# One stage for both input projections, the mixing layer's matrices folded into one, and a dense product with preloaded matrices

## The reference, cut to what matters

```python
xn = _layernorm(x, axis=-1)
x = x + _L0_gnn_ref(xn, edge_index, W, att_src, att_dst, bias) + _L0_mix_ref(xn[None], ...)[0]

def _L0_gnn_ref(x, ...):
    h = (x @ W).reshape(N, 4, 64)
    a_src = jnp.sum(h * att_src[None], axis=-1)
    a_dst = jnp.sum(h * att_dst[None], axis=-1)
    ...   # attention over the edges, + bias, relu

def _L0_mix_ref(x, ...):                 # 8 heads of 32, rank 4
    h = layernorm(x, ln1_g, ln1_b)
    xm = h @ Wx + bx                     # 256 x 256
    q = softmax(xm @ Wq, axis=-1)        # per head, 32 x 4
    k = softmax(xm @ Wk, axis=-2)
    v = xm @ Wv                          # per head, 32 x 32
    attn = (q @ (k.T @ v)) @ Wo + bo
    fx = attn + x
    h2 = layernorm(fx, ln2_g, ln2_b)
    m = gelu(h2 @ W1 + b1) @ W2 + b2     # 256 x 1024, 1024 x 256
    return m + fx
```

## Time and profile before

| | us |
|---|---|
| median of three runs | 5163.15 |
| lowest, highest | 5148.55, 5177.3 |
| the profiled execution | 5160.48 |
| its span (first to last instruction) | 5158.8 |
| busy in it: PE, PEld | 4545.8, 4131.4 |
| busy in it: DVE, ACT, POOL | 3174.7, 2848.2, 1417.0 |

### The profile page before, as it was taken

One profiled execution on the slowest core, in us unless ns is written; L12 is line 12 of the kernel. 1 busy time (PEld: TensorE's weight loads), 2 busy tenths in 40 slices (PEclk: granted clock), 3 DMA queues, 4 the chain that ended last, 5 costly groups with the idle time before them and its releaser, 6 DMA issues. The chain is left out here.

```text
span 5158.8 us, 91254 instructions
## 1 busy us (share of the span) xinstructions
PE 4545.8 (88%) x34042; PEld 4131.4 (80%) x34042; DVE 3174.7 (62%) x2705; ACT 2848.2 (55%) x3889; POOL 1417.0 (27%) x1134
## 2 busy tenths in 40 slices
PE   3555668999999769987799999989999999799989
PEld 3443457999999769964599999978999999688755
DVE  6884322888788531126388888844888888255323
ACT  2662223777777433323077787753778777344332
POOL 0001000122122012210136656640666666100000
PEclk9776779999999789988899999999999999899989
DMA  3881011333333155540144344422443443454100
GB/s 93 137 135 20 3 44 26 97 98 98 86 96 94 56 175 185 184 135 11 39 114 103 101 102 106 103 68 76 105 106 93 106 106 94 118 135 111 29 17 20
DMA packets 199348, 467.51 MB, mean 91 GB/s; under 512 B 108564, under 2 KB 145951, under 8 KB 177016
## 3 DMA queue, kind: packets, MB, share of 16 engines
q1 hardware_dynamic: 179120, 428.36, 32.9%
q0 software_dynamic: 14016, 28.15, 2.2%
q10 hardware_dynamic: 5879, 6.17, 0.4%
HBM read 389.74 MB, written 72.83 MB: 90 GB/s over the span
## 5 line engine op out<-in xcount | busy, mean ns | idle before, releaser
L1161 PE MATMUL g2a_pso<-HX,g2a_wt 125*125 125x129 f32 x5000 | 603.4, 274 | 8.2 <-ACT g2a_wt L1045 4.4
L1161 PE MATMUL g1a_pso<-HX,g1a_wt 125*125 125x129 f32 x5000 | 602.7, 274 | 4.4 <-ACT g1a_wt L1045 3.3
L1161 PE MATMUL g0a_pso<-HX,g0a_wt 125*125 125x65 f32 x5000 | 593.5, 273 | 4.7 <-ACT g0a_wt L1045 3.3
L1161 PEld LDWEIGHTS g0a_pso<-HX,g0a_wt 125*125 125x125 f32 x5000 | 583.6, 193 | 5.0 <-ACT g0a_wt L1045 3.5
L1161 PEld LDWEIGHTS g2a_pso<-HX,g2a_wt 125*125 125x125 f32 x5000 | 576.8, 189 | 8.9 <-ACT g2a_wt L1045 4.8
L1161 PEld LDWEIGHTS g1a_pso<-HX,g1a_wt 125*125 125x125 f32 x5000 | 576.4, 189 | 4.9 <-ACT g1a_wt L1045 3.5
L1045 ACT ACTIVATE g0a_wt<-g0a_pst 125x1000 f32<-125x1000 f32 (+1 forms) x300 | 312.0, 1040 | 197.9 <-PE g0a_pst L1148 197.9
L978 DVE SCALAR_TENSOR_TENSOR g0a_x<-g0a_als,g0a_cd,HX 125x3125 f32<-125x3125 f32 x100 | 347.5, 3475 | 108.5 <-PE g0a_pst L1148 99.3
L978 DVE SCALAR_TENSOR_TENSOR g2a_x<-g2a_als,g2a_cd,g2a_as 125x3125 f32<-125x3125 f32 x100 | 357.7, 3577 | 83.2 <-PE g2a_pst L1148 73.2
L978 DVE SCALAR_TENSOR_TENSOR g1a_x<-g1a_als,g1a_cd,g1a_as 125x3125 f32<-125x3125 f32 x100 | 358.3, 3583 | 81.1 <-PE g1a_pst L1148 70.6
L1045 ACT ACTIVATE g1a_wt<-g1a_pst 125x1000 f32<-125x1000 f32 (+1 forms) x300 | 312.2, 1041 | 169.2 <-PE g1a_pst L1148 169.2
(11 more groups left out here) (463 smaller groups left out, 8141.9 us busy)
## 6 DMA issues: line engine op xcount, KB each, us to landing
g0a_nl<-lowered SPq DMA_DIRECT2D x50, 1367.2 KB
g1a_nl<-lowered SPq DMA_DIRECT2D x50, 1367.2 KB
g2a_nl<-lowered SPq DMA_DIRECT2D x50, 1367.2 KB
moe_wa<-in_L_ffn_W SPq DMA_DIRECT2D x56, 1024.0 KB, 4.9
lowered<-counts_nl SPq DMA_DIRECT2D x25, 1367.2 KB
g3a_nl<-lowered SPq DMA_DIRECT2D x25, 1367.2 KB
g0a_nl<-lowered SPq DMA_DIRECT2D x50, 158.7 KB
g1a_nl<-lowered SPq DMA_DIRECT2D x50, 158.7 KB
```

Source lines behind the costliest of these rows:

```text
L1161: last = nc.tensor.matmul(pso[0:R, unit(q, 0, k) % 2, 0:F + 1], wt[:, side, j * R:(j + 1) * R], HX[:, a, q * HG + k % HG, :], start=(a == ...
```

## The change

- `stage_front` replaces st0, nm0, g0p, st1, nm1, xm and mixp. Each tile is normalised and turned once and multiplied with two matrices: the attention projection (264 columns) and one folded matrix for q, k and v (320 columns). Folded means: Wx times the block matrix of Wq, Wk, Wv (laid out by the host, `c_mixw`), with ln1's gain put on its rows; bx and ln1's shift go through the same matrices into a bias row `bm`. The second layer norm's division is a factor per row (`again`), which VectorE applies when it reads PSUM. The product of the matrices is taken on the chip, 8 matmuls of 320 columns, once.
- q, k and v lie in one tensor `MIX[125, 25, 321]` (before: QK and V).
- The stage mixo also takes the statistics of the sums as they come, and its SP queue issues the loads of W1 and W2.
- `stage_dense_product` replaces nm2, ar0 and mlp: it normalises and turns groups of five tiles ahead, and two groups' hidden layers are computed before the first outputs. W1 and W2 are there already. The two adds to X stand on VectorE behind the normalising of the first two groups. Loops are written out.

```diff
@@ stage_mix, last stage @@
-        stage_small_product(nc, m, "mixo", QK[:, :, 0:J], J, [(0, KVO[:]), (J, a["L0_mix_bo"].unsqueeze(0))], XN)
+        with Stage(nc, "mixo") as s:
...
+                sm.load(sp)
+                for dst, src in ahead:
+                    sp.dma_start(dst, src).then_inc(ahead_in, 16)
...
+            @block.vector
+            def _(dve):
+                for t in range(T):
+                    sm.add(dve, [t])
+                    nc.vector.drain()
+                    sums.take(t, XN[:, t, :])
+                sums.finish(dve)
@@ new stage @@
+def stage_front(nc, m, a, g, X, x_in, mean, rstd, again, XN, AL, HX, MIX):
...
+            dve.wait_ge(x_in, 32)
+            for t in range(T):
+                sums.take(t, X[:, t, :])
+            dve.wait_ge(mix_in, 64)
...
+            sums.finish(dve)
+            nc.vector.drain()
+            for t in range(XS):
+                norm(t)
+            dve.wait_ge(joined, 1)
+            for x in range(2):
+                last = nc.vector.tensor_scalar(wm[:, x, :], psm[:, x, 0:W], gb[:, x:x + 1], None, ALU.mult)
+            last.then_inc(wm_ready, 1)
+            dve.wait_ge(gat_in, 48)
...
+            dve.wait_ge(bias_full, 1)
+            nc.vector.tensor_copy(bm[:], psg[0:R, 0, 0:W]).then_inc(wm_ready, 1)
+            nc.vector.drain()
+            dve.wait_ge(bias_in, 16)
+            for t in range(T):
+                if t + XS < T:
+                    norm(t + XS)
+                dve.wait_ge(full, t + 1)
+                nc.vector.scalar_tensor_tensor(out=MIX[:, t, 0:W], in0=psm[0:R, t % RINGS, 0:W], scalar=again[:, t:t + 1], in1=bm[:],
+                                               op0=ALU.mult, op1=ALU.add).then_inc(mix_out, 1)
...
+            def products(t):
+                pe.wait_ge(copied, t + 1)
+                if t >= RINGS:
+                    for out in (mix_out, gat_out, score_out):
+                        pe.wait_ge(out, t - RINGS + 1)
+                for to, right, n in ((psm, wm, W), (psg, wg, HF + SC)):
+                    for c in range(2):
+                        last = nc.tensor.matmul(to[0:R, t % RINGS, 0:n], xs[:, t % XS, c, :], right[:, c, :], start=(c == 0), stop=(c == 1))
+                last.then_inc(full, 1)
...
+            pe.wait_ge(spread_ready, 1)
+            pe.wait_ge(copied_plain, 1)
...
+            turn(0)
+            turn(1)
+            pe.wait_ge(wm_ready, 2)
...
+            for t in range(T):
+                if t + 2 < T:
+                    turn(t + 2)
+                products(t)
...
+            act.wait_ge(joined, 1)
...
+            for t in range(T):
+                act.wait_ge(turned, t + 1)
+                if t >= XS:
+                    act.wait_ge(full, t - XS + 1)
+                nc.scalar.activation(xs[:, t % XS].rearrange("p c n -> p (c n)"), pst[:, t % 2, 0:2 * R], ACT.Copy).then_inc(copied, 1)
@@ new stage, in place of stage_experts @@
+def stage_dense_product(nc, m, a, w1, w2, w_in, ROWS_, mean, rstd, X, layers):
...
+            def norm(j):
+                for k in range(U):
+                    t = j * U + k
+                    if t >= XR:
+                        dve.wait_ge(turned, t - XR + 1)
+                    nc.vector.tensor_scalar(xn[:, t % XR, :], ROWS_[:, t, :], mean[:, t:t + 1], rstd[:, t:t + 1], ALU.subtract, ALU.mult).then_inc(normed, 1)
+            norm(0)
+            norm(1)
+            for j in range(GROUPS_):
+                g = slice(j * U, (j + 1) * U)
+                nc.vector.tensor_tensor(X[:, g, :], X[:, g, :], ROWS_[:, g, :], ALU.add)
+            nc.vector.drain()
+            dve.wait_ge(small_in, 48)
+            for j in range(GROUPS_):
+                g = slice(j * U, (j + 1) * U)
+                nc.vector.tensor_tensor(X[:, g, :], X[:, g, :], b2[:].unsqueeze(1).to_broadcast([R, U, D]), ALU.add)
+            nc.vector.drain()
+            for j in range(GROUPS_):
+                if j + 2 < GROUPS_:
+                    norm(j + 2)
+                for n, c in chunks[2 * j:2 * j + 2]:
+                    fold(n, c)
+                for k in range(U):
+                    t = j * U + k
+                    dve.wait_ge(y_full, t + 1)
+                    nc.vector.tensor_tensor(X[:, t, :], X[:, t, :], psy[0:R, t % 2, 0:D], ALU.add).then_inc(y_free, 1)
...
+            def hidden(j):
+                pe.wait_ge(moved, (j + 1) * U)
+                for n in range(JOBS_):
+                    o, (c0, cn) = n // 2, HALVES[n % 2]
+                    job = j * JOBS_ + n
+                    if job > 3:
+                        pe.wait_ge(h_ready, job - 3)
+                    for c in range(2):
+                        last = nc.tensor.matmul(psh[:, job % 4, 0:cn], w1[:, c, o * P:(o + 1) * P], xT[:, j % 2, c, c0:c0 + cn], start=(c == 0), stop=(c == 1))
+                    last.then_inc(h_full, 1)
+            def product(j, k):
+                t = j * U + k
+                if k == 0:
+                    pe.wait_ge(h_ready, (j + 1) * JOBS_)
+                if t > 1:
+                    pe.wait_ge(y_free, t - 1)
+                for c in range(MH):
+                    last = nc.tensor.matmul(psy[0:R, t % 2, 0:D], hT[:, j % 2, c, k * R:(k + 1) * R], w2[:, c, :], start=(c == 0), stop=(c == MH - 1))
+                last.then_inc(y_full, 1)
+            for k in range(U):
+                turn(k)
+            pe.wait_ge(w_in, 32)
+            hidden(0)
+            for k in range(U):
+                turn(U + k)
+            hidden(1)
+            for j in range(GROUPS_):
+                for k in range(U):
+                    product(j, k)
+                    if j + 2 < GROUPS_:
+                        turn((j + 2) * U + k)
+                if j + 2 < GROUPS_:
+                    hidden(j + 2)
...
+            act.wait_ge(small_in, 48)
+            for j in range(GROUPS_):
+                for k in range(U):
+                    t = j * U + k
+                    act.wait_ge(turned, t + 1)
+                    for c in range(2):
+                        last = nc.scalar.activation(xT[:, j % 2, c, k * R:(k + 1) * R], pst[:, t % 2, c * R:(c + 1) * R], ACT.Identity,
+                                                    bias=gb[:, 2 + c:3 + c], scale=gb[:, c:c + 1])
+                    last.then_inc(moved, 1)
+                if j > 1:
+                    act.wait_ge(y_full, (j - 1) * U)
+                for n in range(JOBS_):
+                    o, (c0, cn) = n // 2, HALVES[n % 2]
+                    job = j * JOBS_ + n
+                    act.wait_ge(h_full, job + 1)
+                    nc.scalar.activation(hT[:, j % 2, o, c0:c0 + cn], psh[:, job % 4, 0:cn], ACT.Gelu, bias=b1[:, o:o + 1]).then_inc(h_ready, 1)
@@ build @@
-                XT = sb("XT0", [P, 2, N], F32, c1)[:]
+                XN, AGAIN = sb("XN0", [R, T, D], F32, c1)[:], sb("AGAIN0", [R, T], F32, c1)[:]
+                W1, W2, mlp_in = sb("W1", [P, 2, 4 * D], F32, c1)[:], sb("W2", [P, 8, D], F32, c1)[:], nc.alloc_semaphore("mlp_w_in")
+                ahead = [(W1, a["L0_mix_W1"].rearrange("(c p) n -> p c n", p=P)), (W2, a["L0_mix_W2"].rearrange("(c p) n -> p c n", p=P))]
                 with ExitStack() as c2:
-                    XN, XM = sb("XN0", [R, T, D], F32, c2)[:], sb("XM0", [P, 2, N], F32, c2)[:]
-                    stage_stats(nc, "st0", X, MEAN, RSTD, x_in)
-                    stage_norm(nc, m, "nm0", X, MEAN, RSTD, XT, out_rows=XN)
-                    stage_gat_project(nc, m, g0, XT, 2, a["L0_gnn_W"], a["L0_gnn_att_src"], a["L0_gnn_att_dst"], a["L0_gnn_bias"], AL, rows_of(g0))
-                    stage_stats(nc, "st1", XN, MEAN, RSTD)
-                    stage_norm(nc, m, "nm1", XN, MEAN, RSTD, XT, affine=a["c_ln1"])
-                    stage_linear(nc, "xm", XT, 2, a["L0_mix_Wx"], a["c_bx"], 2, ACT.Identity, XM)
-                    stage_mix(nc, m, a, XM, XN)
-                    stage_stats(nc, "st2", XN, MEAN, RSTD)
-                    stage_norm(nc, m, "nm2", XN, MEAN, RSTD, XT, affine=a["c_ln2"])
-                    stage_add_row(nc, "ar0", [a["L0_mix_b2"]], X, more=XN)
-                stage_experts(nc, m, "mlp", 1, XT, None, a["L0_mix_W1"].unsqueeze(0), a["c_mlp_b1"], a["L0_mix_W2"].unsqueeze(0), None, X,
-                              [(a[f"L1_gnn_W{n}"], a[f"L1_gnn_a_src{n}"], a[f"L1_gnn_a_dst{n}"], WA[n]) for n in (1, 2, 3)])
+                    MIX = sb("MIX", [R, T, 2 * 32 + D + 1], F32, c2)[:]
+                    stage_front(nc, m, a, g0, X, x_in, MEAN, RSTD, AGAIN, XN, AL, rows_of(g0), MIX)
+                    stage_mix(nc, m, a, MIX, XN, MEAN, RSTD, ahead, mlp_in)
+                stage_dense_product(nc, m, a, W1, W2, mlp_in, XN, MEAN, RSTD, X,
```

More of the change, by code:

```diff
@@ L1392, in move, with add @@
             self.nc.scalar.activation(self.qT[0:self.K, g % 3, 0:n], self.pst[0:self.K, g % 2, 0:n], ACT.Copy).then_inc(self.moved, 1)
-    def add(self, dve):
-        for t in range(T):
+    def add(self, dve, tiles=range(T)):
```

(31 more changed lines are left out.)

193 lines of the change are left out of this document (110 added, 83 removed).

## The result

The changed kernel takes 5018.95 us (median of 4 runs, 5005.29 to 5021.35) against 5157.15 before (a fourth run of the kernel before, 5151.16 us, joins the three above): ratio 0.9722, 95% interval [0.9699, 0.9746]. The forecast was 5020 in 5001 to 5052. The profiled execution is the fastest of the four, 5005.29 us, span 5003.6.

The account below looks back on a forecast made before the run. Barrier-separated stages run one after another, so each costs its own length. Front -90.7, output product -8.5 and dense -43.7 sum to -142.9: 5160.48 to 5017.6, plus 2.7 for the median, 5020 us; range 5001 to 5052.

Parts of the forecast that it names:

- dense: group 0, cold: Dense stage: group 0's hidden layer starts at a low clock and takes 20.0 us, against 17.0 for later groups.
- dense: wait before group 1: Dense stage: TensorE waits 4.3 us for group 1's ten copies, queued on ScalarE behind group 0's Gelus.
- The front's tile: Front loop: TensorE takes 2.19 us a tile, from the third attention layer's projection rows; VectorE and ScalarE hidden.
- upper bound of 2.5: Front loop: up to 2.5 us a tile if three waits a tile leave TensorE idle, +8 us in all.
- The range: Whole kernel, 5001 to 5052 us: forecast -15 for cheaper heads and run spread, +20 for front bound and cold group 1, and rival 1.
- the dense head: Dense stage, from its start T: small loads first used at T + 3.9, ten copies 3.5, done at T + 7.4 us.
- The weights: W1 and W2, issued in the output product: covered by its 31 us; uncovered they would cost up to 8 us.
- Rival 1: Dense stage: group 1 late and cold (+3), later groups' copy waits (+10), weights late (+8): 5041 us; chance 0.09.
- cold group 1: Dense stage: the wait before group 1 lowers the clock, and a second cold start costs 3.0 us; left in the range.
- rival 2: Front loop: stays at 1.2 GHz throughout, +52 us, total 5072; chance 0.05.
- rival 3: Front and dense stages: both stay at 1.2 GHz, sum +81 us, total 5244, slower; chance 0.02.
- Rival 4: Attention stage: time saved is given back there, so the path is not shortened, total 5163 us; chance 0.01.

Follow-up runs that it names:

- experiment 1: Kernel before with only the new front stage, the rest as before: 5059.78 us, ratio 0.9811 to before.
- experiment 10: Kernel after with the statistics of the mixing layer's output in a stage of their own: 5029.22 us, one run.
- experiment 7: Kernel after with the front stage's 264-column product issued twice for each tile: 5027.08 us.
- experiment 8: Kernel after with one more VectorE add of 256 columns for each front tile: 5010.99 us.
- experiment 5: Kernel after with the dense stage's three small loads issued in the stage before, ahead of the matrices: 4993.0 us.
- experiment 3: Kernel after with W1 and W2 loaded in the dense stage behind its small loads, not in the stage before: 4998.16 us.
- experiment 4: Kernel after with group 1's transposes and copies woven into group 0's products, later groups' transposes one product earlier: 5006.16 us.
- experiment 6: Kernel after with the two small products (mixing output, combine stage) contracting over 128 rows, added rows adding nothing: 5008.09 us.
- its repeat: Kernel after, unchanged, run again on another chip: 5001.18 us, ratio 0.9708 to before.
- experiment 2: Kernel after with the old front, so only the output-product sums and the dense part are new: 5102.8 us, ratio 0.9893 to before.
- experiment 11: Kernel after with woven transposes and copies and early small loads only: 4993.56 us, ratio 0.9687 to before.
- experiment 9: The best version: kernel after with woven transposes and copies, early small loads and 128-row small products: 4985.15 us, ratio 0.9675 to before.

## Why the prediction was right, step by step

| step | forecast | measured |
|---|---|---|
| front: head to the first product | 19.1 | 19.35 |
| front: a tile | 2.19 | 2.18 |
| front: first product to the softmax stage | 59.8 | 58.1 |
| front in all | -90.7 | -92.1 (alone: -93.9) |
| softmax stage and output product | -8.5 | -8.4 (statistics apart: +8.8) |
| dense: first hidden matmul | T + 7.5 | T + 9.9 |
| dense: group 0, cold | 20.0 | 19.2 |
| dense: wait before group 1 | 4.3 | 4.25 |
| dense: later waits | 0.9, three times | 0.89, three times |
| dense in all | -43.7 | -42.6 |
| sum, by stage lengths | -142.9 | -143.1 |
| fall of the median | 143.2 (5163.15 to 5020) | 138.2 (5157.15 to 5018.95) |

- **The stage lengths agree by the mechanism, the total partly by luck.** The runs of either kernel spread by 16 us and more, and the fourth run moved the median before by 6. The profiled pair fell by 155.2, the medians by 138.2. That 5018.95 lies 1 us from 5020 is not a measure of how good the sum is.
- **The front's tile** came from a row of another stage, and experiments 7 and 8 show that TensorE alone sets it, as the sum assumed. My upper bound of 2.5 did not occur, and it rested on a misreading: 1.17 us a tile of the old projection holds its cold start, and TensorE's one wait there is the 9.2 us at the head. At full clock two of its tiles' weight loads recur every 2.03 us, 1.02 a tile, so 0.12 over its columns. Two smaller slips change nothing: 1.75 / 2064 is 0.848 ns, and (31.1 - 3) / 25 is 1.12 us a tile, not 1.16.
- **The range** I gave, 5001 to 5052, is wider than its terms, which make 5005 to 5041; what was measured lies in both.
- **One term was mis-sized**, the dense head: I gave b2's load 3.0 us from its issue, from the earlier trace rows; here it was used 4.9 us after (537.09 to 541.99). The ten copies behind it took 4.1, not 3.5. Experiment 5 gains 4.0 by moving the loads. A cold start 0.8 us cheaper than forecast offset a part.
- **The weights** I called hidden, with up to 8 if uncovered. Hidden was right; experiment 3 puts the price at 3.
- **Rival 1** did not come: later groups waited 0.89. Of its cold group 1, experiment 10's run shows the 3 us that I had left in the range, and experiment 4 removes the wait ahead of it.
- **Rivals 2 and 3** did not come: the front is at 0.54 in 420 to 425 and at 1.00 from 425, and the dense stage stands at 0.96. The front's loop is no test of pauses between groups, nor is the projection in the earlier trace rows: TensorE idled in neither loop. What spoke for rival 2, the output product at the low clock, has a cause that the front lacks: with its rows filled the product rises to 1.00 (experiment 6).
- **Rival 4's place**, the attention layer, does move, but nothing ties that to the change. Its profiled lengths are 830.2 to 830.4 us (after, its repeat, experiments 1, 2, 5 and 7; experiment 3 the same, 830.3) or 843.4 to 853.2 (before, experiments 4, 6, 8 to 11). The profiled run of after had the short form, which fits its 5005 beside 5018 to 5021 in the three others, of which there is no profile. Their mean clocks point the same way: 0.939 against 0.932 to 0.934. What decides the form in an execution is open; I made no run for it. In the best version, all of whose runs lie within 12 us, the profiled one had the long form, so an influence of the kernel is not excluded. It bears on the 155.2 us between the two profiled runs (13 of them), not on the stage lengths in the table.

## What to carry to other kernels

When every stage ends at a barrier, a merged stage can be sized by itself: passes times columns times the rate of a row at full clock, plus a head counted instruction by instruction. After such a merge look at the head first, at small loads and at copies queued behind other work on ScalarE; reordering them took 10 us off the stage here without a new instruction. Where a stage shows TensorE fully busy at half clock, look at how many rows its matmuls fill, as in experiment 6, before calling it bound. And compare stage lengths where single executions of a kernel differ by 15 us.

## What the runs showed of the hardware

- TensorE was 5.00 of 5 us busy with 33-row matmuls and stayed at a granted clock of 0.50 for the whole product; with rows that add nothing, up to 128, it came to 1.00. The 8-row product went from 629 ns a pass to 379 by the same edit.
- The first attention layer, with a 3.3 us wait of TensorE near its middle, took 13 to 23 us more in the profiles in which the clock stayed at 0.50 for longer after its start and after that wait. In experiment 9's profile TensorE was busy 25.00 of 25 us at 0.50 behind the wait:

```profile
1145.40:1170.40 25.00, 25.00 (x122) 25.00 (x121) 10.99 (x7) 9.78 (x12) 1.15 (x3) 0.50 0.25 63
```
